# Expert stages: the turns and scatters of a quad move between the experts of the next quad, and the scatter runs in three bfloat16 terms

## The reference

```python
capacity = int(Sz * 2.0 / E) + 1                       # 65 of 256 tokens, 8 experts
scores = softmax(einsum('bsd,ed->bse', x, router_w))
gate_vals, sel_idx = top_k(swapaxes(scores, 1, 2), capacity)
tokens = x[b_idx, sel_idx]                             # gather
h = gelu(einsum('becd,edh->bech', tokens, w1) + b1)    # 128 -> 512
y = einsum('bech,ehd->becd', h, w2) + b2               # 512 -> 128
gated = y * gate_vals[..., None]
out = zeros_like(x).at[b_idx, sel_idx].add(gated)      # scatter, then x = x + out
```

## Time and profile before

| | |
|---|---|
| median of 3 runs | 3567.07 us (3566.18 to 3569.9) |
| the profiled execution | 3569.11 us, its span 3567.3 us |
| mean granted TensorE clock | 0.907 of full speed |
| busy: TensorE, VectorE, ScalarE, GpSimd | 87%, 66%, 48%, 34% |
| opening of the first quad, first stage | 593.23 us |
| opening of the second to fourth quad | 640.53, 684.95, 729.37 us |
| opening of the last quad | 907.04 us |
| last instruction of the first expert stage | 953.31 us |

### The profile page before, as it was taken

The page is one execution under the profiler, slowest core; times in us unless marked ns, Lnnn a source line. Parts: engine busy times, 40 slices in busy tenths (PEclk is TensorE's granted clock), DMA queues, the critical chain, the costliest instruction groups (busy, mean ns, idle before and its releaser), DMA issues. The chain is left out here.

```text
span 3567.3 us, 49293 instructions
## 1 busy us (share of the span) xinstructions
PE 3112.0 (87%) x16500; PEld 2058.4 (58%) x16500; DVE 2343.9 (66%) x5381; ACT 1722.8 (48%) x3723; POOL 1199.0 (34%) x1206
## 2 busy tenths in 40 slices
PE   6999974999872999997579998788889999999989
PEld 2455564888641444444568886676635555555557
DVE  4888875555564777775845553003579999999964
ACT  2444322333341899997133332212356666666644
POOL 3444420000122777775100000001234444444432
PEclk9999966999995999999589996557999999999999
DMA  3000011111032101101221100000000000000001
GB/s 111 1 1 1 1 39 66 37 37 34 17 118 77 30 25 30 30 27 37 62 75 37 45 1 1 0 0 26 1 1 1 1 1 1 1 1 1 1 8 41
DMA packets 106555, 91.23 MB, mean 26 GB/s; under 512 B 15501, under 2 KB 96147, under 8 KB 104000
## 3 DMA queue, kind: packets, MB, share of 16 engines
q1 hardware_dynamic: 104928, 87.25, 7.7%
q10 hardware_dynamic: 1376, 0.82, 0.1%
HBM read 57.60 MB, written 30.15 MB: 25 GB/s over the span
## 5 line engine op out<-in xcount | busy, mean ns | idle before, releaser
L2370 ACT ACTIVATE m_x_hT<-m_x_hid,wm_b 128x260 f32<-128x260 f32 x512 | 242.6, 477 | 433.5 <-PE m_x_hid L2292 433.5
L1319 POOL TENSOR_TENSOR c_tE<-c_tE,c_tDm 128x256 f32<-128x256 f32 x512 | 372.2, 728 | 139.5 <-ACT c_tE L1279 125.7
L1202 DVE TENSOR_REDUCE c_tM<-c_tpa 128x2 f32<-128x512 f32 x512 | 330.0, 681 | 130.9 <-PE c_tpa L1104 129.9
L1279 ACT ACTIVATE c_tE<-c_tpb 128x512 f32<-128x512 f32 x512 | 309.8, 606 | 43.3 <-PE c_tpb L1121 43.3
L2292 PE MATMUL m_x_hid<-m_x_xg,wm_w 128*128 128x260 f32 x1024 | 306.2, 386 | 8.9 <-ACT m_x_hT L2370 5.4
L2300 PE MATMUL m_x_yp<-m_x_hT,wm_w 128*128 128x260 f32 x1024 | 300.7, 383 | 0.0
L1655 POOL TENSOR_TENSOR b_wkv<-b_at,b_rec 128x512 f32<-128x512 f32 x128 | 163.1, 1274 | 306.2 <-DVE b_rec L1591 306.2
L1104 PE MATMUL c_tpa<-c_tK,c_Qm 96*128 96x256 f16 x1024 | 204.7, 283 | 49.9 <-DMA c_Qm<-aug_d 36.8
L2148 POOL TENSOR_TENSOR rstd_all<-m_x_vareps,m_x_neg_half 128x8 f32<-128x8 f32 x16 | 26.4, 1647 | 652.7 <-DVE m_x_vareps L2231 652.7
L1260 ACT ACTIVATE c_tDm<-wc_pos,c_LD 128x128 f32<-128x128 f32 x512 | 209.2, 411 | 21.1 <-PEq L96 21.1
L1121 PE MATMUL c_tpb<-c_Qm,c_tK 101*128 101x256 f16 x1024 | 198.2, 275 | 23.8 <-ACT c_tE L1279 23.5
(11 more groups left out here) (335 smaller groups left out, 7463.4 us busy)
## 6 DMA issues: line engine op xcount, KB each, us to landing
m_x_ir<-idx_d SPq DMA_DIRECT2D x16, 1040.0 KB, 6.7
xn_d<-xn SPq DMA_DIRECT2D x32, 256.0 KB, 2.3
m_x_xs<-xn_d SPq DMA_DIRECT2D x16, 512.0 KB, 4.0
c_tK<-k_d SPq DMA_DIRECT2D x32, 192.0 KB
c_Qm<-q_d SPq DMA_DIRECT2D x128, 48.0 KB
wm_w<-in_m_w SPq DMA_DIRECT2D x2, 2048.0 KB, 9.8
gate_d<-c_pgate SPq DMA_DIRECT2D x16, 256.0 KB
q_d<-c_phi SPq DMA_DIRECT2D x32, 128.0 KB
```

Of the source, the lines that this page charges most:

```text
L1202: nc.vector.tensor_reduce(out=M[:, u % 2, 2 * h:2 * h + 2], in_=pa[:, h % 2], axis=AX.X, op=ALU.max).then_inc(s["max_done"], 1)
L1279: nc.scalar.activation(E[:, h % 8].rearrange("p a q -> p (a q)"), pb[:, h % 2, :], ACT.Exp).then_inc(s["exp_done"], 1)
L1319: nc.gpsimd.tensor_tensor(diag, diag, Dm[:, u % 2, h:h + 1, :].to_broadcast([P, 2, P]), ALU.mult).then_inc(s["dmul_done"], 1)
L2370: nc.scalar.activation(hT[:, e % 2, j, :], hid[:, c % 2, 0:QW], ACT.Gelu, bias=w["m_b1"][:, c:c + 1]).then_inc(s["gelu_done"], 1)
```

## The change

- The turns and scatters of quad q-1 now stand between the experts of quad q, on TensorE and VectorE: turns of batches 0, 1, 2, 3 ahead of experts 0, 1, 3, 4 (`TURNS`), scatters ahead of experts 2, 4, 5, 6 (`OUTS`). The loop runs one pass longer (NQ + 1), and the last pass holds the turns and scatters of the last quad alone. A table `ring` numbers the uses of the four `misc` banks in the new order.
- `sel` is a bfloat16 0/1 matrix. The gate is multiplied in when the turned `y` is read from PSUM. The product is kept as three bfloat16 terms: `turned` on VectorE writes the first term and the rest in fp32 (five and five instructions per batch, for the two copies of before), `rest_parts` on GpSimd writes the second and the third term. `scatter` sums 3 x 5 x 2 = 30 bfloat16 matmuls.
- `select` of a batch comes as five instructions together, at experts 0 to 3 of the following quad; `bn`, `moments` and `inverse` of quad q-2 (before: q-1) run in quad q, the first two an expert earlier.
- `yT` has two slots, `ys` three. What the loads wait for stays the same event: the eighth gather of quad q-2.

The diff, cut to its core; the other hunks write the numbers of `ring` in place of those of `first_unit`:

```diff
-        yT = sb("yT", [P, QB, NE, CAP])
-        ys = sb("ys", [CH, 2, NCH, D])
-        sel = sb("sel", [CH, QB, NCH, T])
+        yT = sb("yT", [P, 2, QB, NE, CAP])
+        YS = 3
+        ys = sb("ys", [CH, YS, 3, NCH, D], BF16)
+        rest = sb("rest", [CH, YS, NCH, D])
+        sel = sb("sel", [CH, QB, NCH, T], BF16)
...
+        TURNS = {0: 0, 1: 1, 3: 2, 4: 3}
+        OUTS = {2: 0, 4: 1, 5: 2, 6: 3}
...
+            def load(q, slot):
+                if q >= 2:
+                    sp.wait_ge(s["misc"], ring["g", q - 2, 7] + 1)
```

GpSimd:

```diff
+            def rest_parts(q, b):
+                n = q * QB + b
+                pool.wait_ge(s["misc_free"], ring["t", q, b, 1] + 1)
+                nc.gpsimd.tensor_copy(ys[:, n % YS, 1], rest[:, n % YS]).then_inc(s["mid_part"], 1)
+                pool.wait_ge(s["mid_part"], n + 1)
+                nc.gpsimd.tensor_tensor(ys[:, n % YS, 2], rest[:, n % YS], ys[:, n % YS, 1], ALU.subtract).then_inc(s["last_part"], 1)
...
-            for q in range(NQ):
+            for q in range(NQ + 1):
                 if q + 2 < NQ:
                     low_part(q + 2, q % 2)
-                inverse(q)
+                if q > 0:
+                    rest_parts(q - 1, 0)
+                    rest_parts(q - 1, 1)
+                if q > 1:
+                    inverse(q - 2)
+                if q > 0:
+                    rest_parts(q - 1, 2)
+                    rest_parts(q - 1, 3)
+            inverse(NQ - 1)
```

VectorE:

```diff
+                if e == 0 and q >= 2:
+                    dve.wait_ge(s["misc"], ring["t", q - 2, QB - 1, 1] + 1)
...
+            def select(q, b):
+                if q > 0:
+                    dve.wait_ge(s["misc"], ring["o", q - 1, b] + 1)
+                for c in range(NCH):
+                    nc.vector.tensor_scalar(sel[:, b, c, :], steps[0:CH, :], cols[:, 1, c, bass.ds(q * QB + b, 1)], None, ALU.is_equal)\
+                        .then_inc(s["sel_done"], 1)
+
+            def turned(q, b, part):
+                n = q * QB + b
+                c0, c1 = split[part]
+                dve.wait_ge(s["misc"], ring["t", q, b, part] + 1)
+                if part == 0 and n >= YS:
+                    dve.wait_ge(s["misc"], ring["o", (n - YS) // QB, (n - YS) % QB] + 1)
+                    dve.wait_ge(s["last_part"], n - YS + 1)
+                y = lambda c: misc[0:CH, bank("t", q, b, part), (c - c0) * D:(c - c0 + 1) * D]
+                gate = lambda c: cols[:, 0, c, n:n + 1]
+                for c in range(c0, c1):
+                    nc.vector.tensor_scalar(ys[:, n % YS, 0, c, :], y(c), gate(c), None, ALU.mult).then_inc(s["first_part"], 1)
+                for c in range(c0, c1):
+                    dve.wait_ge(s["first_part"], n * NCH + c + 1)
+                    m = nc.vector.scalar_tensor_tensor(out=rest[:, n % YS, c, :], in0=y(c), scalar=gate(c), in1=ys[:, n % YS, 0, c, :],
+                                                       op0=ALU.mult, op1=ALU.subtract)
+                m.then_inc(s["misc_free"], 1)
+
+            def out(q, b):
+                dve.wait_ge(s["misc"], ring["o", q, b] + 1)
+                xb = k.X[:, bass.ds((q * QB + b) * 2, 2), :].rearrange("p a d -> p (a d)")
+                nc.vector.tensor_tensor(xb, misc[:, bank("o", q, b), 0:2 * D], xb, ALU.add).then_inc(s["misc_free"], 1)
...
+            def quad(q):
+                u = q % 2
+                if q + 1 < NQ:
                     onehot(q + 1, 1 - u, 0)
                 for e in range(NE):
-                    if not first and e in (1, 2):
-                        bn(q - 1, (e - 1) * QB, e * QB)
-                    if not first and e == 3:
-                        moments(q - 1)
-                    if not last and e % 2 == 0 and e // 2 + 1 < QB:
+                    if q > 1 and e in (0, 1):
+                        bn(q - 2, e * QB, (e + 1) * QB)
+                    if q > 1 and e == 2:
+                        moments(q - 2)
+                    if q + 1 < NQ and e % 2 == 0 and e // 2 + 1 < QB:
                         onehot(q + 1, 1 - u, e // 2 + 1)
-                    if not last:
-                        take(1 - u, e, number + e)
-                    for m in range(QB * NCH * e // NE, QB * NCH * (e + 1) // NE):
-                        select(q, m)
-                    y_out(q, e)
-                tail(q, number if last else number + 8)
+                    if q + 1 < NQ:
+                        take(q + 1, e)
+                    if q > 0 and e < QB:
+                        select(q - 1, e)
+                    if q > 0 and e in TURNS:
+                        turned(q - 1, TURNS[e], 0)
+                        turned(q - 1, TURNS[e], 1)
+                    if q > 0 and e in OUTS:
+                        out(q - 1, OUTS[e])
+                    if q < NQ:
+                        y_out(q, e)
```

TensorE:

```diff
+            def turn(q, b, part):
+                if b == 0 and part == 0:
+                    pe.wait_ge(s["y_done"], (q + 1) * NE)
+                free("t", q, b, part)
+                c0, c1 = split[part]
+                for c in range(c0, c1):
+                    mm = nc.tensor.transpose(misc[0:CH, bank("t", q, b, part), (c - c0) * D:(c - c0 + 1) * D],
+                                             yT[:, q % 2, b, :, :].rearrange("p e c -> p (e c)")[:, c * CH:(c + 1) * CH], k.ident[:])
+                mm.then_inc(s["misc"], 1)
+
+            def scatter(q, b):
+                n = q * QB + b
+                free("o", q, b)
+                pe.wait_ge(s["sel_done"], (n + 1) * NCH)
+                pe.wait_ge(s["first_part"], (n + 1) * NCH)
+                pe.wait_ge(s["last_part"], n + 1)
+                for h in range(2):
+                    for part in range(3):
+                        for c in range(NCH):
+                            mm = nc.tensor.matmul(misc[:, bank("o", q, b), h * D:(h + 1) * D], lhsT=sel[:, b, c, h * P:(h + 1) * P],
+                                                  rhs=ys[:, n % YS, part, c, :], start=(part == 0 and c == 0),
+                                                  stop=(part == 2 and c == NCH - 1))
                 mm.then_inc(s["misc"], 1)
...
+            def quad(q):
+                u = q % 2
+                if q < NQ:
+                    for j in range(NJH):
+                        up(q, u, 0, j, q > 0)
                 for e in range(NE):
-                    if not last:
-                        gather(q + 1, 1 - u, e, number + e, True)
-                    for j in range(NJH):
+                    if q + 1 < NQ:
+                        gather(q + 1, e)
+                    if q > 0 and e in TURNS:
+                        turn(q - 1, TURNS[e], 0)
+                        turn(q - 1, TURNS[e], 1)
+                    if q > 0 and e in OUTS:
+                        scatter(q - 1, OUTS[e])
+                    for j in range(NJH if q < NQ else 0):
                         if e + 1 < NE:
                             up(q, u, e + 1, j, True)
-                        down(q, e, j, not first)
-                pe.wait_ge(s["y_done"], (q + 1) * NE)
...
+                        down(q, e, j, q > 0)
```

More of the change, by code:

```diff
@@ L2122, in _ @@
             for q in range(4):
-                load(q, q % 2, q)
+                load(q, q % 2)
                 if q == 1:
@@ L2128, in _ @@
                 for u in range(2):
-                    load(i * 2 + u, u, 4)
+                    load(i * 2 + u, u)
             begin_loads(nc, arrive, loads)
@@ L2254, in _ @@
                     onehot(0, 0, unit // 2 + 1)
-                take(0, unit, unit)
+                take(0, unit)
             dve.wait_ge(s["cols_ps"], 1)
@@ L2258, in _ @@
             dve.wait_ge(s["cols"], 1)
-            quad(0, 0, True, False)
-            quad(1, 1, False, False)
-            for i in range(1, NQ // 2 - 1):
-                for u in range(2):
-                    quad(i * 2 + u, u, False, False)
-            quad(NQ - 2, 0, False, False)
-            quad(NQ - 1, 1, False, True)
+            for q in range(NQ + 1):
+                quad(q)
             bn(NQ - 1, 0, W2)
@@ L2270, in _, with free, gather @@
         def _(pe):
-            def gather(q, slot, unit, number, later):
+            def free(*unit):
+                at_least(pe, s["misc_free"], ring[unit] - 3)
+            def gather(q, unit):
                 b, er = unit // 2, unit % 2
+                slot = q % 2
                 n = NE // 2 * CAP
@@ L2303, in down @@
                     mm.then_inc(s["down_done"], 1)
-            def quad(q, u, first, last):
-                number = first_unit(q)
-                for j in range(NJH):
-                    up(q, u, 0, j, not first)
-                for e in range(NE):
-                    if not last:
-                        gather(q + 1, 1 - u, e, number + e, True)
-                    for j in range(NJH):
+            def quad(q):
[3 more added lines that the diff above has]
+                        up(q, u, 0, j, q > 0)
+                for e in range(NE):
```

(8 more changed lines are left out.)

80 lines of the change are left out of this document (24 added, 56 removed).

## The result

The changed kernel takes 3582.2 us (median of 6 runs, 3580.3 to 3585.1), the kernel before 3566.9 us beside it. The ratio is 1.0044, 95% interval 1.0031 to 1.0057: slower, by 0.4%. The forecast was 3579 us, with a chance of 0.60 for slower. The profiled execution has a span of 3579.9 us, 12.6 more than that of before (3567.3).

The account below looks back on a forecast made before the run. TensorE, 87% busy, was taken to bound the kernel. Per stage 62.3 + 8.0 + 7.0 + 27.3 = 104.6 us against 99.8: +4.8, second stage +6.8; 3567.1 + 11.6 = 3578.7, so 3579 us, range 3553 to 3607.

Parts of the forecast that it names:

- turns and scatters, quads 1 to 7: TensorE work placed between experts: 8.9 us per quad, 62.3 us per stage for quads 1 to 7.
- late load, quads 1 to 5: Load issued 1.56 us before the quad opens makes ScalarE's cast wait; TensorE stalls 1.6 us per quad, 8.0 us.
- waits for VectorE at expert 4: TensorE waits for VectorE, slowed beside GpSimd, at expert 4's turn: 1.0 us in seven quads, 7.0 us per stage.
- clock dips behind the load: Rival: TensorE's clock falls at each stall, 1.8 us in ten quads, 18 us, 3597 us; chance 0.05.
- last pass: Last quad's turns and scatters, covered by nothing: VectorE's chain, GpSimd, last scatter and X, 27.3 us per stage.
- quad 0, beyond its tail: First quad of a stage: already has the load wait, so no further cost was forecast, 0 us.
- against the tails: Eight removed tails of turns and scatters per stage, seven of 12.4 us and one of 13.0: 99.8 us gained.
- pitch of 56 ns: Start-to-start time of one bfloat16 scatter matmul on TensorE, giving 6.7 us per quad for 120 matmuls.
- the 98 and 77 ns rivals: Scatter matmuls slower through weight loads: 98 ns gives 3650 us, chance 0.04; 77 ns gives 3614 us, chance 0.06.
- The 0.4 us per quad that the forecast added in the second stage: Longer late-load stall in the second expert stage, 2.0 us instead of 1.6 in quads 1 to 5: 10.0 us.
- the disturbance by GpSimd: VectorE's one-hots and selects stand beside GpSimd's subtraction, up to 1.4 us each; rival without it 3562 us, chance 0.20.
- The prediction's own signs: Period from quad 2 on about 43.5 us; prediction wrong if below 42.5 or above 45, or last pass under 24 us.

Follow-up runs that it names:

- run 1: Changed kernel, each quad's load waiting only for one-hots and low parts of the quad two before, ScalarE's cast taking over the gather wait: 3559.7 us, ratio 0.9976.
- run 2: Kernel before with only its loads released early, by one-hots and low parts, the cast waiting for the gather: 3563.1 us, ratio 0.9988.
- run 3: Changed kernel with the selects of each stage's last quad moved from the last pass into that quad's own experts: 3570.6 us, ratio 1.0006.
- run 8: As run 6, with `bn` and `moments` of the quad before the last moved to expert 7 of the last quad: 3551.0 us, ratio 0.995.
- run 9: Changed kernel with early load and hoisted selects, last quad of each stage scattered in float32 with gated selects, no GpSimd work there: 3533.6 us, ratio 0.991.
- run 10: Changed kernel with early load and hoisted selects, third bfloat16 term left out (20 scatter matmuls, one GpSimd operation per batch): 3497.2 us, ratio 0.9806.
- run 6: Changed kernel with both early load and the last quad's selects moved into its own experts: 3547.6 us, ratio 0.9938.
- run 4: Changed kernel's order with the scatter of the kernel before (float32, gate in selects, no added GpSimd work): 3599.3 us, ratio 1.0096.

## Why the prediction was right

The sum of the first stage, step by step. The measured column counts from start to start, as above, and takes a quad without any wait as 42.15 - 1.03 = 41.1 us (run 1), against 32.0 of experts: 2.2 us of turns, 6.7 of scatters (4 x 30 x 56 ns), and 0.05 us at the first up behind each scatter.

| step | forecast | measured |
|---|---|---|
| turns and scatters, quads 1 to 7 | 62.3 | 9.1 x 6 + 8.7 = 63.4 |
| late load, quads 1 to 5 | 8.0 | 2.0 + 2.0 + 2.1 + 2.5 + 2.9 = 11.5 |
| waits for VectorE at expert 4 | 7.0 | 1.2 (quad 6) + 0.2 x 3 = 1.7 |
| clock dips behind the load | 0 (a rival) | 1.6 x 2 = 3.2 |
| last pass | 27.3 | 26.5 |
| quad 0, beyond its tail | 0 | 2.1 |
| against the tails | 99.8 | 99.9 |
| **sum** | **+4.8** | **+8.5** |

- *Turns and scatters.* The pitch of 56 ns is exact, in runs with 30 and with 20 matmuls. Weight loads of 98 ns are no bound; the 98 and 77 ns rivals are out. By the rule of the Trainium skill ("TensorE: Matmul & The Clock Gate", Back-to-back issue gap), about 81 ns for a stream with its weight loads, thirty would have taken some 2.4 us to the last start, where the trace has 1.62: the trace differs from that figure, and the measurement decides. (Quad 7 gathers nothing and has 28.9 us of experts, 907.04 to 935.90 in the kernel before: 891.47 to 929.05 leaves 8.7.)
- *The late load* was the right mechanism, but it cost 2.0 to 2.1 us in quads 1 to 3 and not 1.6. The forecast let the pause begin at the shown end of the matmul before it (T+5.15, with T the quad's opening); the next matmul was due at T+4.90, and the first up behind the pause loses 0.1 us more. That it grew to 2.5 and 2.9 us in quads 4 and 5 was not foreseen: from the issue of `xs` to the cast went 6.88, 6.86, 6.97, 7.34 and 7.81 us, and why the last two were slower is open. The 0.4 us per quad that the forecast added in the second stage did not come, 10.9 us against 11.5 in the first. Run 1 showed the mechanism by taking it away, run 2 that the kernel before hid it behind its tails.
- *VectorE at expert 4* is the mis-sized term: 1.7 us in place of 7.0. The order of its queue and the disturbance by GpSimd were as reckoned, and without the late load the wait is in every quad from 1 on, 1.0 us as forecast and 7.0 a stage (run 1). But beside the late load only 0.3 us or less of it is left: the pause that holds TensorE gives VectorE the time to catch up. The forecast added two waits of which the first nearly swallows the second.
- *The clock* made up for part of this. It was priced at 1.8 us a dip, as a rival at every pause; 1.6 us came at four of the ten pauses (after 2.19 and 2.67 us, in the second stage after 1.89 and 2.48). Length alone doesn't say which: in run 3 a pause of 2.48 us had no dip and one of 2.01 us had. Quad 0 had one too, after 2.94 us (2.52 and none before), which with its longer pause is its 2.1 us.
- *The last pass* came out at 26.5 for 27.3 us. Its chain was read rightly as VectorE's, and run 3 confirmed it by 6.0 us for 20 selects. What lies under it was not in the prediction: with the selects gone, GpSimd's 2.1 us per batch and the half clock hold the pass at 20 us (run 8). Other operations shorten it: 13.3 us with plain float32 in run 9, 17.7 with one GpSimd operation in run 10.
- The side of the result is therefore earned by the late load and the last pass, and near luck in size: 5.3 us too much on VectorE and 0.8 on the last pass stand against 1.1 too little on turns and scatters, 3.5 on the load, 3.2 on the clock and 2.1 in quad 0. In the second stage the same terms gave +6.1 for +6.8. The prediction's own signs say as much: quads 1 to 3 have the period that it named, but quads 4 and 5 lie above its bound of 45 us and quad 6 below that of 42.5.
- One reading was off without a consequence: the gather's matmuls of the earlier trace rows start 0.111 us apart, not 0.109.

The whole: as it stands the interleaving costs two things that it need not. Turns and scatters cost 63.4 us a stage where seven tails cost 86.9, a gain of 23.5; the last pass gives back 13.5, and the late load with its dips, VectorE's waits and quad 0's longer pause 18.5.

## What to carry to other kernels

When a stretch that bounds the kernel is taken out, look at every transfer and every wait that it used to hide, by the distance from issue to use in the trace, and release the buffer by its last real reader and not by a convenient later event: that alone was worth 22 us here, and 5 us or less in the kernel before. A cheaper operation with a longer chain (copy, split, subtract on another engine) pays where other work covers it and costs where nothing does, so the last round may need the plain form. A pause of one engine gives the others time to catch up, so two waits in a row, for different engines, don't add. And what a wait costs is read from start to start, with and without it: the idle time that the profile shows was 1.72 us where 1.98 were lost, and 0.61 where 1.03 were.

## What the runs showed of the hardware

- VectorE operations on SBUF alone often stand until GpSimd's is through: the addition of 128x8 in `moments` took 0.17 us in the last pass of run 9, where GpSimd was idle, and 1.36 us in the last pass of the changed kernel, ending together with GpSimd's 1.39 us subtraction (mean 0.82 us from 628 to 887 us); a pair of one-hots took 0.87 us in the earlier trace rows and 2.29 us in run 1. The operations that read PSUM (`ys`, `rest`, 338 ns) did not stretch: none of the 640 took over 351 ns.
- GpSimd's cast of 104x640 from float32 to bfloat16 took 0.72 us and its subtraction 1.42 us; my estimates from another copy and a larger subtraction were 1.0 and 1.3.
- TensorE kept its full clock in the last pass of run 9, where no wait was longer than 0.58 us. In run 6 thirty bfloat16 matmuls behind a wait of 4.4 us came at 1.2 GHz, 3.36 us against 1.84. It is not the type: in run 4 twenty float32 instructions behind a wait of 1.98 us took 4.61 us against 2.47.
- What a dip costs was much the same each time: 1.6 us in a quad, 1.5 us in a scatter of thirty.
